# Diff-attention block with feed-forward: output projection in eight slots per tile, later statistics, a quarter of w1 and a pre-cast w2 in the feed-forward

## Reference

```python
sa, ca, ga, sb, cb, gb = chunks of silu(c) @ wmod            # each [1024]; |ga|, |gb| >= 0.25
h = layernorm(x) * (1 + ca) + sa
q, k, v = h@Wq+bq, h@Wk+bk, h@Wv+bv                           # 8 heads of 128
attn = softmax(q k^T / sqrt(128))                             # per head, 4096 x 4096
ao = attn @ v[h % 4] - lam * (attn @ v[h % 4 + 4])            # 4096 x 1024
x1 = x + ga * (0.2 * (layernorm(ao)*ln_w + ln_b) @ Wo + bo)
h2 = layernorm(x1) * (1 + cb) + sb
out = x1 + gb * (gelu(h2 @ w1 + b1) @ w2 + b2)                # 1024 -> 4096 -> 1024
```

## Time and profile before

| | |
|---|---|
| median of 3 runs | 2591.47 us (2590.08 to 2784.51) |
| profiled execution | 2590.08 us, span of its slowest core 2588.5 us |
| spans of the eight cores | 2576.9 to 2588.5 us, mean granted clock 0.976 to 0.979 |
| busy TensorE | 2374.2 us, 92% |
| busy ScalarE | 1432.7 us, 55% |
| busy VectorE | 675.9 us, 26% |
| busy GpSimd | 322.7 us, 12% |
| on the chain that ended last | TensorE 82%, DMA 6%, VectorE 5%, ScalarE 3% |

### The profile page before, as it was taken

How to read it: one execution, slowest core, us unless ns; L and a number is a source line. 1 busy time by engine, 2 the same in 40 slices (tenths; PEclk the granted TensorE clock), 3 DMA queues, 4 the chain that set the end, 5 groups by cost and what they waited for, 6 DMA issues and landing times.

```text
span 2588.5 us, 43437 instructions; the slowest of 8 cores (2576.9 to 2588.5 us)
## 1 busy us (share of the span) xinstructions
PE 2374.2 (92%) x17364; PEld 1317.9 (51%) x17364; DVE 675.9 (26%) x1207; ACT 1432.7 (55%) x1567; POOL 322.7 (12%) x294
## 2 busy tenths in 40 slices
PE   2578999999999999999999995689999999999999
PEld 1233666666665665666566662244444444444444
DVE  2443221212222222211256665612010110201101
ACT  2432888888888898989877774450312213021130
POOL 1211000000000000000054453431010100101000
PEclk9889999999999999999999997899999999999999
DMA  9513111110111000002266667681020110201001
GB/s 211 159 46 49 22 24 23 26 22 9 26 22 26 6 9 9 9 5 36 47 132 150 142 144 186 186 187 49 33 82 17 65 50 33 82 17 65 33 33 41
DMA packets 119539, 162.74 MB, mean 63 GB/s; under 512 B 37728, under 2 KB 86956, under 8 KB 118320
## 3 DMA queue, kind: packets, MB, share of 16 engines
q1 hardware_dynamic: 80528, 123.80, 15.3%
q0 software_dynamic: 38672, 35.65, 10.3%
q10 hardware_dynamic: 144, 0.52, 0.1%
HBM read 145.27 MB, written 50.34 MB: 76 GB/s over the span
## 4 chain that ended last, share of the span: by engine, by line
PE 82%; DMA 6%; DVE 5%; issue 3%; ACT 3%; SPq 1%; POOL 0%; DVEq 0%; ACTq 0%; POOLq 0%
PE bk L192 41%; PE sc L192 40%; DMA aoR<-ao_scr 3%; DMA wm<-wmod 1%; ACT h_bf L199 1%; DVE bst L700 1%; DMA x_scr<-xo 1%; DVE bst L296 1%; DVE qS L207 1%; DVE bst L298 1%; ACT h2T L199 1%; ACT expT L199 1%; PE bk L196 1%; SPq L64 0%; DVE rec L549 0%
## 5 line engine op out<-in xcount | busy, mean ns | idle before, releaser
L199 ACT ACTIVATE expT<-sc,Bneg 128x1024 bf16<-128x1024 f32 x1024 | 1092.1, 1120 | 205.5 <-PE sc L192 195.2
L192 PEld LDWEIGHTS bk<-v_aug,expT 128*128 128x128 bf16 x8192 | 543.1, 98 | 245.3 <-issue 31.0
L192 PE MATMUL bk<-v_aug,expT 128*128 128x129 bf16 x8192 | 640.8, 221 | 10.7 <-DVE ao_ch L203 5.2
L192 PE MATMUL sc<-qS,kS 128*128 128x512 bf16 x2048 | 609.2, 379 | 1.3 <-ACT expT L199 0.5
L199 ACT ACTIVATE g<-sc,vecT 128x512 bf16<-128x512 f32 x256 | 175.9, 687 | 650.1 <-PE sc L192 650.1
L192 PE MATMUL sc<-h2F,w_sb 128*128 128x512 bf16 x2048 | 444.1, 379 | 0.0
L192 PEld LDWEIGHTS sc<-h2F,w_sb 128*128 128x128 bf16 x2048 | 200.6, 98 | 242.0 <-issue 1.0
L192 PE MATMUL bk<-hT,Wre 128*128 128x512 bf16 x768 | 231.2, 379 | 9.7 <-DVE nmx L500 2.8
L192 PE MATMUL bk<-w2hi,g 128*128 128x512 bf16 x768 | 173.6, 379 | 0.0
L192 PE MATMUL bk<-w2lo,g 128*128 128x512 bf16 x768 | 173.6, 379 | 0.0
L203 POOL TENSOR_TENSOR x1f<-x1f,gbb 128x1024 f32<-128x1024 f32 x32 | 75.1, 2349 | 739.9 <-DMA x1f<-x_scr 739.9
(11 more groups left out here) (138 smaller groups left out, 1512.9 us busy)
## 6 DMA issues: line engine op xcount, KB each, us to landing
xr<-x SPq DMA_DIRECT2D x32, 512.0 KB, 6.6
xo<-x SPq DMA_DIRECT2D x32, 512.0 KB, 4.4
x_scr<-xo SPq DMA_DIRECT2D x32, 512.0 KB, 5.8
x1f<-x_scr SPq DMA_DIRECT2D x32, 512.0 KB, 4.3
out<-x1f SPq DMA_DIRECT2D x32, 512.0 KB, 2.9
wms<-wmod POOLq DMA_DIRECT2D x8, 1024.0 KB, 10.6
ao_scr<-ao_ch SPq DMA_DIRECT2D x32, 256.0 KB, 2.6
w_sb<-w POOLq DMA_DIRECT2D x16, 512.0 KB, 8.9
```

Source lines behind the costliest of these rows:

```text
L192: return p.op("tensor", lambda e: e.matmul(out, lhsT, rhs, start=start, stop=stop, skip_group_check=True), waits, sig)
L199: return p.op("scalar", lambda e: e.activation(out, in_, fn, bias=bias, scale=scale), waits, sig)
```

## The change

1. `o_tile` has eight slots. In order: mm; mm + evac; xg, norm2 of tile t-2, load of x for t+3; Ta(t+1); mm and stats_ao(t+1); mm + evac; Th for tile t-3; stats_x1(t-1). `seg` 3 to 7 run four tiles each, so 22 tiles are in attention and 10 in the tail. The fill has a slot in every group.
2. Five `xo`, four `aoR`, four `tmp`; the added ones lie where the last quarter of w1 lay (`RX`). `ao_scr` loads run up to three tiles ahead.
3. In the tail both adds are on GpSimd and norm2 alternates between VectorE and ScalarE.
4. w1 is four tiles `w1q`; 12 loads are issued in attention (every 18 groups), the last four in the first feed-forward block at mt = 4, after the last statistics and transposes of the projection (`o_rest`, also moved there).
5. w2 is cast DRAM to DRAM by 16 GpSimd DMAs spread over segments 8 to 23; the feed-forward's copy is 8 plain loads of 1 MB on SyncE, issued at mt = 4 of the first block instead of 16 casting ones during and after the tail.

The core of the diff:

```diff
-    xo = [at("xo%d" % i, H, F32, RW + 16384 + 4096 * i) for i in range(3)]
-    tmp = [at("tmp%d" % i, 512, F32, RW + 28672 + 2048 * i) for i in range(2)]
-    aoR = [at("aoR%d" % i, H, BF16, SL[2] + 2048 * i) for i in range(2)]
+    RX = R0 + 49152
+    xo = [at("xo%d" % i, H, F32, RW + 16384 + 4096 * i if i < 3 else RX + 4096 * (i - 3))
+          for i in range(5)]
+    tmp = [at("tmp%d" % i, 512, F32, RW + 28672 + 2048 * i if i < 2 else RX + 8192 + 2048 * (i - 2))
+           for i in range(4)]
+    aoR = [at("aoR%d" % i, H, BF16, SL[2] + 2048 * i if i < 2 else RX + 12288 + 2048 * (i - 2))
+           for i in range(4)]
...
+    def o_load_ao(upto):
+        while n_ao[0] <= min(upto, NT - 1):
+            t = n_ao[0]
+            m = 8 * 3 + 2 * (t // 8)
+            if m + 1 not in ao_tok:
+                return
+            ao_ld[t] = p.dma("sync", aoR[t % 4][:, :], ao_scr[t * 128:(t + 1) * 128, :],
+                             "ar%d" % (t % 4),
+                             [ao_tok[m], ao_tok[m + 1], Ta_pe.get(t - 4), aos_tok.get(t - 4),
+                              wo_tok["w"]])
+            n_ao[0] += 1
...
+        x, n = xo[t % 5], 2 * (t % 2) + ch
+        free[b] = stt(tmp[n][:, :], bank(b), rsB[t % 4][:, 0:1], ga_b[:, cs],
+                      ALU.mult, ALU.mult, [k, rs_tok[t], tmp_tok[n], wo_tok["ga"]])
+        tmp_tok[n] = x1_tok[(t, ch)] = tt(x[:, cs], x[:, cs], tmp[n][:, :], ALU.add,
+                                          [free[b], xg_tok[t]], eng=eng)
...
+    def o_late(t, cfg, banks):
+        if t >= 3:
+            o_Th((t - 3) // 2, (t - 3) % 2, next(banks), cfg[4][t % 2])
     def o_tile(t, banks, cfg):
...
         b = next(banks)
         o_mm(t, 0, b, range(4))
         if t >= 1:
             o_store_x1(t - 1)
-        if t + 2 < NT:
-            o_load_ao(t + 2)
+        o_load_ao(t + 3)
         yield
         o_evac(t, 0, b, o_mm(t, 0, b, range(4, 8)), x1_eng[0])
         yield
         if t + 1 < NT:
             o_xg(t + 1)
+        if t >= 2:
+            o_norm2(t - 2, n2_eng[t % 2])
+        if t + 3 < NT:
+            o_load_x(t + 3)
         yield
         if t + 1 < NT:
             o_Ta(t + 1, next(banks), copy_eng)
         yield
-        if t >= 1:
-            o_norm2(t - 1, n2_eng)
-        if t + 2 < NT:
-            o_load_x(t + 2)
-        yield
         b = next(banks)
         o_mm(t, 1, b, range(4))
+        if t + 1 < NT:
+            o_stats_ao(t + 1, on)
         yield
         o_evac(t, 1, b, o_mm(t, 1, b, range(4, 8)), x1_eng[1])
         yield
-        if t + 2 < NT:
-            o_stats_ao(t + 2, on)
-        yield
-        if t >= 2:
-            o_Th(t // 2 - 1, t % 2, next(banks), th_eng)
-        yield
-        o_stats_x1(t, on)
-        yield
-    w1_sb = at("w1_sb", KT * FF, BF16, R0)
-    w1_pe = [None]
-    def load_w1(n):
-        cs = slice(n * 256, (n + 1) * 256)
-        p.dma("gpsimd", w1_sb[:, :].rearrange("p (k f) -> p k f", k=KT)[:, :, cs],
-              w1_d[:, :].rearrange("(k p) f -> p k f", p=128)[:, :, cs],
-              "w1%d" % (n // 4), [w1_pe[0]])
+        o_late(t, cfg, banks)
+        yield
+        if t >= 1:
+            o_stats_x1(t - 1, on)
...
+    w1q = [at("w1q%d" % q, KT * 1024, BF16, R0 + 16384 * q) for q in range(4)]
+    def load_w1(n, waits):
+        p.dma("gpsimd", w1q[n // 4][:, :].rearrange("p (k f) -> p k f", k=KT)
+              [:, :, n % 4 * 256:(n % 4 + 1) * 256],
+              w1_d[:, :].rearrange("(k p) f -> p k f", p=128)[:, :, n * 256:(n + 1) * 256],
+              "w1%d" % (n // 4), waits)
+    def cast_w2(n):
+        p.dma("gpsimd", w2_scr[256 * n:256 * (n + 1), :], w2_d[256 * n:256 * (n + 1), :], "wc",
+              [p.last("pe")])
...
-    TAIL = ("scalar", ("gpsimd", "vector"), "scalar", "scalar", "scalar")
+    V2, S2 = ("vector", "vector"), ("scalar", "scalar")
+    IN_ATT = ("gpsimd", ("gpsimd", "gpsimd"), "vector", V2, V2)
+    TAIL = ("scalar", ("gpsimd", "gpsimd"), "scalar", ("vector", "scalar"), S2)
...
-            n = 2 if pos == 2 else 1 if 2 < pos < 31 else 0
+            n = 2 if pos == 2 and seg > 2 else 1
...
-                k = 2 if seg == 2 else 3
+                k = 2 if seg == 2 else 4
...
-        if seg >= 0 and g >= 25 * NT and (g - 25 * NT) % 14 == 7 and g < NG:
-            load_w1((g - 25 * NT) // 14)
+        if 8 * NT <= g < 24 * NT and g % NT == 20:
+            cast_w2(m - 8)
+        if 25 * NT <= g < NG and (g - 25 * NT) % 18 == 9 and (g - 25 * NT) // 18 < 12:
+            load_w1((g - 25 * NT) // 18, [w1_pe])
...
-        half, o = (w2lo, w2hi)[n // 8], (2 * n) % 16
-        p.dma("gpsimd", half[:, :].rearrange("p (k n) -> p k n", k=16)[:, o:o + 2, :],
-              w2_d[:, :].rearrange("(k p) n -> p k n", p=128)[:, 2 * n:2 * n + 2, :],
-              "w2%d" % (n // 4), [k_att])
+        half, o = (w2lo, w2hi)[n // 4], (4 * n) % 16
+        p.dma("sync", half[:, :].rearrange("p (k n) -> p k n", k=16)[:, o:o + 4, :],
+              w2_scr[:, :].rearrange("(k p) n -> p k n", p=128)[:, 4 * n:4 * n + 4, :],
+              "w2%d" % (n // 2), [k_att, p.last("wc")])
...
-        if t % 2 == 0:
-            load_w2(n_w2)
-            n_w2 += 1
     o_store_x1(NT - 1)
-    o_norm2(NT - 1, "scalar")
-    for f in range(2):
-        o_Th(NT // 2 - 1, f, next(banks), "scalar")
-    while n_w2 < 16:
-        load_w2(n_w2)
-        n_w2 += 1
-    k_w1 = [p.last("w1%d" % q) for q in range(4)]
-    k_w2 = [p.last("w2%d" % q) for q in range(4)]
+    o_norm2(NT - 2, "vector")
+    o_stats_x1(NT - 1, "gpsimd")
+    o_norm2(NT - 1, "vector")
+    def o_rest():
+        for t in range(NT, NT + 3):
+            o_late(t, TAIL, itertools.repeat(7))
...
+            if b == 0 and mt == 4:
+                o_rest()
+                o_end = [p.last("pe"), p.last("dve"), p.last("pl"), p.last("act")]
+                o_st = [st_tok[t] for t in range(NT - 5, NT)]
+                for n in range(12, 16):
+                    load_w1(n, o_end + o_st)
+                for n in range(8):
+                    load_w2(n)
+                k_w1 = [p.last("w1%d" % q) for q in range(4)]
+                k_w2 = [p.last("w2%d" % q) for q in range(4)]
+                k_gb = p.dma("sync", gb_b[:, :], g_scr[1, :].partition_broadcast(128), "ga",
+                             o_end + [g_tok[6], g_tok[7]])
+                k_b2 = p.dma("sync", gbb2[:, :], b2_d[:].partition_broadcast(128), "bo", o_end)
+                k_gbb2 = tt(gbb2[:, :], gbb2[:, :], gb_b[:, :], ALU.mult, [k_gb, k_b2],
+                            eng="gpsimd")
...
-                       [free[ub], k_h2F[b], k_w1[mt // 8]] if kt == 0 else (), sig=kt == KT - 1)
+                       [free[ub], k_h2F[b], p.last("w1%d" % (mt // 8))] if kt == 0 else (),
+                       sig=kt == KT - 1)
```

More of the change, by code:

```diff
@@ L108, in build_nc @@
     g_scr = nc.dram_tensor("g_scr", [2, H], F32, kind="Internal").ap()
+    w2_scr = nc.dram_tensor("w2_scr", [FF, H], BF16, kind="Internal").ap()
     h2T_scr = nc.dram_tensor("h2T_scr", [NC, 128, KT * CW], BF16, kind="Internal").ap()
@@ L678, in build_nc @@
         {} for _ in range(10))
-    tmp_tok = [None, None]
+    tmp_tok = [None] * 4
     ln2_tok, aos_tok, ao_ld, x_ld = {}, {}, {}, {}
     nmC = [const("nmC%d" % i, 1, F32) for i in range(2)]
[L683 to L687, removed]
+    n_ao = [0]
+    def o_load_ao(upto):
[9 more added lines that the diff above has]
+            n_ao[0] += 1
     def o_load_x(t):
-        x_ld[t] = p.dma("sync", xo[t % 3][:, :], x_d[t * 128:(t + 1) * 128, :], "xo%d" % (t % 3),
-                        [st_tok.get(t - 3), h2_tok.get(t - 3), wo_tok["w"]])
+        x_ld[t] = p.dma("sync", xo[t % 5][:, :], x_d[t * 128:(t + 1) * 128, :], "xo%d" % (t % 5),
+                        [st_tok.get(t - 5), h2_tok.get(t - 5), wo_tok["w"]])
     def o_xg(t):
-        xg_tok[t] = tt(xo[t % 3][:, :], xo[t % 3][:, :], gabo[:, :], ALU.add,
+        xg_tok[t] = tt(xo[t % 5][:, :], xo[t % 5][:, :], gabo[:, :], ALU.add,
                        [x_ld[t], wo_tok["ga"]], eng="gpsimd")
@@ L724, in o_norm2 @@
         if eng == "vector":
-            h2_tok[t] = ts(h2[t % 4][:, :], xo[t % 3][:, :], mv[:, 0:1], rs[:, 0:1],
+            h2_tok[t] = ts(h2[t % 4][:, :], xo[t % 5][:, :], mv[:, 0:1], rs[:, 0:1],
                            ALU.subtract, ALU.mult, w)
@@ L734, in o_Ta @@
         for kt in range(KT):
-            k = tr(bank_bf(b)[:, kt * 128:(kt + 1) * 128], aoR[i][:, kt * 128:(kt + 1) * 128],
+            k = tr(bank_bf(b)[:, kt * 128:(kt + 1) * 128], aoR[t % 4][:, kt * 128:(kt + 1) * 128],
                    [free[b], ao_ld[t]] if kt == 0 else (), sig=kt == KT - 1)
@@ L855, in prep67 @@
         yield from wo_prep()
-    IN_ATT = ("gpsimd", ("gpsimd", "gpsimd"), "vector", "vector", "vector")
-    TAIL = ("scalar", ("gpsimd", "vector"), "scalar", "scalar", "scalar")
+    V2, S2 = ("vector", "vector"), ("scalar", "scalar")
+    IN_ATT = ("gpsimd", ("gpsimd", "gpsimd"), "vector", V2, V2)
```

(14 more changed lines are left out.)

21 lines of the change are left out of this document (8 added, 13 removed).

## The result

The changed kernel takes 2570.74 us in the median of four runs against 2591.2 us; the ratio of comparable runs is 0.9921, 95% interval 0.9899 to 0.9944. So it is faster by 0.8%, 20 us, and the forecast was 2567 us. Its profiled execution took 2570.62 us with a span of 2569.1 us on its slowest core (core 7), against 2588.5 us of before. Some executions of all these kernels are slower on one die or both; ratios compare the others.

What follows compares the result with a forecast made beforehand. The prediction took attention to be bound by TensorE and the tail by latency. Segments +42, tail with `o_rest` -76.5 and late loads +11.6 gave -23 us against 2590.08: 2567 us, range 2530 to 2600.

Steps and rivals of the forecast that it cites:

- the equal packet counts: First feed-forward block, while w1 and w2 load: queues q0 and q1 alternate by packet, so their counts match.
- a wait of 1 us for the aoT copy: Attention, each tile: TensorE's first Wo matmul of half 1 waits about 1 us for VectorE's aoT copy.
- Five tiles into attention: Attention segments with four tiles: VectorE's latency stalls TensorE, 12.7 us a tile, +42 us (27 to 66).
- The tail: Ten projection tiles after attention: loads are ahead, engines decide, 6.9 us a tile, 69.5 us to the feed-forward's first matmul.
- The half-speed start: Tail: after TensorE idles over 3 us once a pair of tiles, slower matmuls add 0.65 us a pair.
- `o_rest`: First feed-forward block, before mt 4: TensorE waits for the last tile's h2 and a bank 7 read-out, +5.3 us.
- The late loads: First feed-forward block, mt 24: TensorE waits for the last w1 quarter, +10.6 us (+6 to +25), +1 for half speed.
- both end together: First feed-forward block: w1's 4 x 1024 and w2's 8 x 512 packets alternate and finish at the same time.
- the w1 quarter in time: Rival, first feed-forward block: w1's late quarter arrives before mt 24 needs it, total 2555 us, chance 0.17.
- VectorE eating the gain: Rival, attention: a stall of 2.5 us a tile gives 2591 us, no change; chance 0.12.
- neither stall is there: Rival: VectorE's queue in attention is shorter, the tail runs at 6.0 us, w1 comes in time; 2531 us, chance 0.12.
- The clock at attention's tiles: Rival: waits inside attention tiles drop TensorE's granted clock, +36 us there, +18 in the tail, 2621 us; chance 0.06.

Runs made afterwards that it cites:

- experiment 4: The changed kernel with attention's norm2 queued on VectorE behind the aoT copy, where GpSimd's add already runs: 2575.85 us, ratio 0.9944 to the kernel before.
- experiments 5, 6: Each on the changed kernel: w2 by GpSimd's casting loads again, no DRAM cast (2572.21 us); two ao buffers, loads two tiles ahead (2571.32 us).
- experiment 8: All tail norm2 on VectorE, against the ten-slot, three-tile version with w1 before w2, three `o_rest` banks, two early w2 loads: 2530.86 us, 0.975 to the kernel before.

## Why the prediction was right

The total was forecast at -23 us and measured at -20. That it came so close is luck. The signs of the terms were right, but their sizes were off by -14 us (segments, with `seg` 2: 28 for 42), -7 (tail with `o_rest`: -83 for -76.5) and +24 (late loads with the clock: 35.5 for 11.6), and that cancelled to 3. Of the signs that the prediction named for being right, the equal packet counts appeared, for 30 us, and no wait for ao_scr stood on the chain; stores 51 to 52 us apart (48.3), a wait of 1 us for the aoT copy (0.2), 65 to 72 us from attention's last matmul to the first of w1 (61) and a wait near 10 us at mt 24 (31) did not. The terms:

- *Five tiles into attention*: forecast +42, measured +25.5 for the segments. The work per slot was right (11.45 us a tile; the segment without stalls 45.8), the stall was mis-sized: 1.3 us a tile in the hand schedule, some 0.5 measured (48.3 - 45.8 less the segment's end, over four). The step that failed is norm2 at the 2.18 us of the earlier trace rows. That row held for a start inside GpSimd's add; moved ahead of GpSimd's work, it takes 0.80 (experiment 4). The wait for the aoT copy was forecast at 1.0 us and is 0.2; the one before Th, 0.3, is 0.3.
- *The tail*: forecast 69.5 us after 151.3, counted from attention's last matmul; measured from the last store, 58.9 after 149.0, so -90.1 in place of -81.8. A tile takes 5.9 us, where the sum for VectorE gave 6.0, but that sum had norm2 at 2.18: VectorE is busy 49.0 us of the ten tiles, 4.9 each, and GpSimd 48.1. So it isn't VectorE's work that sets the pace; TensorE's waits in the tail are for ScalarE's `h` and `aoT` (3.69 us the longest), and what the bound is no run shows. The half-speed start was put at every pair; in this execution two pairs of four have it (3.28 and 3.35 us for eight matmuls in place of 1.89). "Without w2's casts and with four `aoR`, the loads are ahead" holds in the main: taking either back costs the tail 15 and 12 us on the slowest core (experiments 5, 6). The reading that the old chain was mostly loads of ao_scr was too strong: they are 54 us of it, and stores of x1 another 19. What I hadn't seen is that tiles at this pace nearly fill the DMA engines: 0.98 in the two tiles shown, 0.79 over the whole tail.
- *`o_rest`*: forecast +5.3, measured 6.8, by the waits named.
- *The late loads*: forecast +10.6 and +1 for the clock, measured +31.0, and 4.5 for the rest of the stage, which is half-speed stretches after the waits (160 matmuls in 37.26 us and 64 in 16.50, 2.6 and 2.5 us over full speed) less one that the kernel before had at the start. The mechanism is the one forecast. Its size failed in two steps. A pair was priced 0.17 us; the view of the two queues of the changed kernel from 1680 to 1690 us gives more:

```profile
q1 hardware_dynamic: 915, 1.82, 62.9%
q0 software_dynamic: 916, 0.46, 44.3%
```

  915 w2 packets and 916 w1 packets, 0.629 x 160 / 915 + 0.443 x 160 / 916 = 0.11 + 0.077 = 0.187 us a pair. That is the quickest stretch: from 1670 to 1680 us it is 754 and 752 packets, 0.213 us a pair, and over the 40 us from 1660 on 3261 w1 packets passed, one in 0.196 us on each of the 16 engines. And "both end together" left out what stands behind w2 on SyncE. The same view from 1700 to 1710 us:

```profile
q1 hardware_dynamic: 835, 2.31, 69.2%
q0 software_dynamic: 713, 0.36, 32.9%
```

  w2 is nearly through (its last load was issued at 1681.1 and landed 30 to 32 us later), the packets beside w1's are now 2.8 KB in the mean, up to 8 KB, and w1's last 900 take 19 us beside those. Nor did w1 start together with w2: its first load was issued at 1653.93, but no q0 packet passed before 1660, when h2T's cheap packets, for which 3.5 us had been taken off, were through. From first issue to last landing w1 took 65.2 us, where 43.0 were forecast; the slower turns make about 5 of the difference, the last 900 packets 9, the start 3 and the h2T store 3.5. The issues of that stretch, with the median time to landing in the last column:

```profile
w2lo<-w_scr SPq DMA_DIRECT2D x4, 1024.0 KB, 20.4
w2hi<-w_scr SPq DMA_DIRECT2D x4, 1024.0 KB, 32.8
w1q<-w POOLq DMA_DIRECT2D x4, 512.0 KB, 42.9
x1f<-x_scr SPq DMA_DIRECT2D x3, 512.0 KB, 22.9
...
h2F<-h2T_scr SPq DMA_DIRECT2D x1, 1024.0 KB, 25.1
gb_b<-g_scr SPq DMA_DIRECT2D x1, 512.0 KB, 28.1
```

  w1's four loads land 42.9 us after issue in the median, the last 62.4. w2, needed later, lands in 20.4 and 32.8 in the median of its halves.

Of the rivals, the w1 quarter in time did not happen, nor VectorE eating the gain. Of "neither stall is there" two parts of three came: the stall in attention was small and the tail ran at 5.9 us a tile, but w1 was late. The clock at attention's tiles did not fall: 1.00 over the five segments. (That rival's +36 counts one half-speed stretch a tile where its text says two; nothing hung on it.) The estimate by the Trainium skill's page DMA: Bandwidth & Descriptors, section Anatomy of one DMA, had w1 in time; the measured 62.4 us decide against it for two busy queues. The rule that does describe it is on the same page, section Queues, rings and completion order: each engine goes round the queues that have work, one packet at a time. The equal counts, 915 and 916, agree. What the page calls a packet holds several descriptors, what the profile counts is one row of a transfer, and whether a turn is one row or several these counts don't tell.

## What to carry over

- A load that is needed soon and is cut into small packets is better not run beside bulk loads on another queue: here holding w2 back until w1 had landed moved no byte and gave 28 us, and what stands behind the bulk load in its queue counts too.
- Work moved under another stage has to be weighed against what it costs in its old place once that place is repaired: the old tail took 9.9 us a tile, the new one 4.5 for one more, and attention charges 6.5.
- A duration read from a row belongs to what ran beside it. Ask for each moved operation on VectorE whether GpSimd will already be running when it starts.

## What the runs showed of the hardware that was not expected

- norm2 (128x1024 float32 to bfloat16 on VectorE) takes 0.80 us if it starts ahead of GpSimd's two-input add. If it starts inside one it takes 2.0 to 2.6 us in attention (experiment 4) and mostly 1.7 to 1.9 in the tail of experiment 8. In the first case GpSimd's half add takes 1.70 in place of 1.27 us; an add of 128x1024 behind a norm2 that still ran took 2.79 in place of 2.35 (experiment 8).
- w1's cast packets of 512 B pass at 1520 in 5 us on an otherwise empty set of engines, and at 709 to 916 in 10 us beside a queue of mostly 2 KB packets. From 1670 to 1700 us the counts of both sides are within 2% (752 and 754, 916 and 915, 884 and 865); at the two ends they are not (709 and 862, 713 and 835).
- In the tail, eight Wo matmuls took 3.28 us behind a wait of 3.69 us, at a granted clock of 0.55 (mostly the lower of the two levels, 1.2 GHz), and 1.89 us behind one of 1.10 us, at 1.00 (2.4 GHz). Two more waits lie between: behind 2.52 us it was 3.35 us at 0.54, and behind 1.82 us, at the tail's end, the first w1 matmuls ran at 1.00. The timeline of TensorE in the changed kernel:

```profile
1589.93 0.55 PE L197 MATMUL bk<-ident_b,h 128*128 128x128 bf16 x7 [3.69 <-ACT h L200]
1590.84 3.28 PE L193 MATMUL bk<-Wo_sb,aoT 128*128 128x512 bf16 x8 [0.36 <-ACT aoT L200]
...
1626.05 0.55 PE L197 MATMUL bk<-ident_b,h 128*128 128x128 bf16 x7 [1.10 <-ACT h L200]
1626.95 1.89 PE L193 MATMUL bk<-Wo_sb,aoT 128*128 128x512 bf16 x8 [0.36 <-ACT aoT L200]
```

  Each pair of rows is the second part of a set of transposes with the wait ahead of it, and the Wo matmuls behind.
